# Marks of the alignment path: two accumulated TensorE products and a ScalarE copy in place of a VectorE difference and shuffle

## What is computed

```python
# 1  attention with squared scores, 16 heads of 16
A = tril((q * 0.25) @ k.T) ** 2 ;  o = (A @ v) / (A.sum(-1) + 1e-5) ;  x += o @ Wo
# 2  alignment of the context (77 rows) to the normalized x (1024 rows)
D = pairwise_euclidean(ctx, norm(x))
R[i, j] = D[i, j] + min(R[i-1, j], R[i, j-1], R[i-1, j-1])
path = backtrack(R)                 # from (76, 1023) to (0, 0): diagonal, up or left
x[j] += sum of ctx[i] over the cells (i, j) of the path
# 3  feed-forward: 256 -> 1024, two ten-stage butterflies, gelu, 1024 -> 256
x += ffn(norm(x))
```

## Time and profile before

| | us |
|---|---|
| median of three runs | 914.62 |
| the profiled execution | 919.23 |
| its span, first to last instruction | 917.5 |
| TensorE busy | 782.3 |
| VectorE busy | 489.3 |
| ScalarE busy | 446.9 |

### The profile page before, as it was taken

One profiled execution on the slowest core, in us unless ns is written; L12 is line 12 of the kernel. 1 busy time (PEld: TensorE's weight loads), 2 busy tenths in 40 slices (PEclk: granted clock), 3 DMA queues, 4 the chain that ended last, 5 costly groups with the idle time before them and its releaser, 6 DMA issues.

```text
span 917.5 us, 12051 instructions
## 1 busy us (share of the span) xinstructions
PE 782.3 (85%) x3927; PEld 384.2 (42%) x3927; DVE 489.3 (53%) x1921; ACT 446.9 (49%) x672; POOL 147.5 (16%) x332
## 2 busy tenths in 40 slices
PE   4887988799899978899988978867899972699998
PEld 3352323234333324333233322334476561457657
DVE  5637553531546122569997884239759886431000
ACT  1245776766667754778865757523412300241220
POOL 2121222221221111212222202101001000100100
PEclk9899997889999989979999989977999986799999
DMA  4481532210323220314422211101010012000001
GB/s 145 146 251 65 184 108 77 69 48 23 116 70 149 71 59 20 89 34 137 132 90 84 61 39 34 25 9 28 15 38 31 15 45 64 10 0 24 24 0 46
DMA packets 52761, 61.25 MB, mean 67 GB/s; under 512 B 21007, under 2 KB 31939, under 8 KB 52699
## 3 DMA queue, kind: packets, MB, share of 16 engines
q1 hardware_dynamic: 51611, 56.28, 20.4%
q0 software_dynamic: 1088, 4.19, 1.4%
HBM read 37.16 MB, written 23.30 MB: 66 GB/s over the span
## 4 chain that ended last, share of the span: by engine, by line
PE 57%; DVE 29%; ACT 6%; issue 5%; DMA 2%; SPq 1%; DVEq 0%; ACTq 0%
PE psO L1205 11%; PE psS L1188 10%; PE psS L1352 8%; PE psW L1362 7%; PE psW L1257 5%; DVE FOLD L917 3%; DVE STATS L1032 3%; PE psW L1248 3%; PE psW L1280 3%; ACT ARENA L778 3%; DVE FOLD L977 3%; PE psW L1264 2%; PE psW L1289 2%; DVE XX L1053 2%; PE psW L1292 2%
## 5 line engine op out<-in xcount | busy, mean ns | idle before, releaser
L778 ACT ACTIVATE ARENA<-psS 128x1024 f32<-128x1024 f32 (+3 forms) x384 | 301.0, 811 | 110.5 <-PE psS L1188 107.7
L1188 PE MATMUL psS<-ARENA 96*128 96x512 bf16 (+3 forms) x768 | 196.2, 347 | 30.5 <-ACT ARENA L778 29.5
L702 POOL TENSOR_SCALAR_AFFINE_SELECT ARENA<-ARENA 128x256 f32<-128x256 f32 x256 | 110.4, 435 | 410.3 <-ACT ARENA L778 408.6
L1205 PE MATMUL psO<-ARENA 128*32 128x512 f32 (+3 forms) x1536 | 173.2, 525 | 3.4 <-ACT ARENA L783 2.5
L1188 PEld LDWEIGHTS psS<-ARENA 96*128 96x128 bf16 x768 | 57.1, 100 | 219.3 <-ACT ARENA L778 125.7
L1362 PE MATMUL psW<-W2E,ARENA 128*128 128x256 f32 x512 | 114.6, 385 | 6.8 <-DVE ARENA L1168 6.2
L1362 PEld LDWEIGHTS psW<-W2E,ARENA 128*128 128x128 f32 x512 | 98.7, 193 | 23.0 <-DVE ARENA L1168 6.6
L845 ACT ACTIVATE ARENA<-psS,BEFF 128x512 f32<-128x512 f32 x64 | 43.5, 687 | 122.7 <-PE psS L1352 122.7
L1248 PE MATMUL psW<-IDENT,XX 128*128 128x128 f32 x192 | 36.9, 348 | 46.8 <-DVE XX L1053 46.8
L1080 DVE TENSOR_TENSOR X<-X,psW 128x512 f32<-128x512 f32 x32 | 21.7, 684 | 100.6 <-PE psW L1280 50.6
L1257 PE MATMUL psW<-XX,ARENA 128*128 128x512 f32 x128 | 68.0, 638 | 5.1 <-DVE ARENA L1068 3.1
(11 more groups left out here) (143 smaller groups left out, 817.9 us busy)
## 6 DMA issues: line engine op xcount, KB each, us to landing
ARENA<-qk_parts SPq DMA_DIRECT2D x192, 128.0 KB, 2.7
qk_parts<-ARENA SPq DMA_DIRECT2D x16, 768.0 KB, 3.7
out<-ARENA SPq DMA_DIRECT2D x16, 256.0 KB, 2.1
X<-in_x POOLq DMA_DIRECT2D x3, 1024.0 KB, 7.2
dist<-ARENA SPq DMA_DIRECT2D x1, 2560.0 KB, 8.1
MORE<-dist SPq DMA_DIRECT2D x16, 160.0 KB, 2.3
path<-MORE SPq DMA_DIRECT2D x16, 80.0 KB, 2.0
path<-FOLD SPq DMA_DIRECT2D x16, 80.0 KB, 2.2
```

Of the source, the lines that this page charges most:

```text
L702: pool.affine_select(out=blk, in_=blk, compare_op=ALU.is_ge, fill=0.0, base=0, pattern=[[0, 2], [1, P]], channel_multiplier=-1).then_inc(s ...
L778: nc.scalar.activation(A[:, (2 * G + a) % A_PAIRS, :, 0:N], psS[:, a, :, 0:N], ACT.Square).then_inc(s_sq, 1)
L1188: ins = nc.tensor.matmul(psS[:, a, j, 0:N], KST[0:STACK, g % 2, 2 * a + j, kt * P:(kt + 1) * P], QST[0:STACK, g % 2, 2 * a + j, q0:q0 + N] ...
L1205: ins = nc.tensor.matmul(psO[32 * j:32 * j + 32, o % 2, q0 - qc * HALF:q0 - qc * HALF + N], V1[:, kt, GH * g + j], A[:, (2 * G + j // 2) % ...
```

## The change

`mark` on VectorE keeps only the first of its three operations. UPTO is doubled, so that two groups alternate. A new unit `("mark", w, g)` joins the plan and `ITEM_KINDS`. TensorE multiplies UPTO with MIRRORED[:, 0] and REACH with MIRRORED[:, 1] into one psW bank, accumulating: MIRRORED is the identity for lanes 0 to 63 and reverses the blocks in each set of 32 of the other lanes, with +1 for the first and -1 for the second matrix. ScalarE copies lanes 0 to 63 as they are and lanes 64 to 127 with reversed columns into MARK, and SP sends all lanes with one DMA. TURNED goes. A `mark` unit stands four backward steps after the step that completes its group, the last one directly after it, and the late half of the path (`path(w, 1)`) is loaded after backward step 4 instead of 8. GpSimd makes MIRRORED at the start, by seven instructions.

```diff
@@ make_plan
-                      + [("backward", w, t) for t in reversed(range(early, T))] + path(w, 1)
-                      + [("backward", w, t) for t in reversed(range(early))] + path(w, 0))
+                      + flat([("backward", w, t)] + ([("mark", w, t // GRP + 1)] if t % GRP == GRP - 4 and t + GRP < T else [])
+                             + (path(w, 1) if t == GRP - 4 else []) for t in reversed(range(T))) + [("mark", w, 0)] + path(w, 0))
-ON_SCALAR = ("turn_x", "qk", "value", "turn_s", "turn_f", "dist")
+ON_SCALAR = ("mark", "turn_x", "qk", "value", "turn_s", "turn_f", "dist")
+ITEM_KINDS = (..., "out", "mark")
@@ SyncE, path_out
-                sp.wait_ge(s_path, w * T // GRP + n + 1)
-                for lanes, marks in ((slice(0, 64), MARK), (slice(64, 128), TURNED)):
-                    sp.dma_start(by_lane(path_dram, w)[lanes, g * GRP:(g + 1) * GRP], marks[lanes, n % 2]).then_inc(s_path_out[w][n % 2], 16)
+                sp.wait_ge(s_free[bank("mark", w, g)], made("mark", w, g))
+                sp.dma_start(by_lane(path_dram, w)[:, g * GRP:(g + 1) * GRP], MARK[:, n % 2]).then_inc(s_path_out[w][n % 2], 16)
@@ GpSimd, lane_tables
+                step(pool.memset(MIRRORED[:], 0.0))
+                for x in range(2):
+                    step(pool.affine_select(out=MIRRORED[0:64, x, 0:64], ..., fill=1.0 - 2.0 * x, ...))
+                    for q in range(PAIR, 2 * PAIR):
+                        step(pool.affine_select(out=MIRRORED[lanes, x, lanes], ..., fill=1.0 - 2.0 * x, base=1 - W_BLK, ...))
@@ ScalarE
+                elif kind == "mark":
+                    ...
+                    act.wait_ge(s_ready, ready(*u))
+                    marks = psW[:, bank(*u), 0:GRP * CB].rearrange("p (t c) -> p t c", t=GRP)
+                    nc.scalar.activation(MARK[0:64, n % 2], marks[0:64], ACT.Copy)
+                    nc.scalar.activation(MARK[64:128, n % 2][:, :, ::-1], marks[64:128], ACT.Copy).then_inc(s_free[bank(*u)], 1)
@@ VectorE, backward
+                if n % GRP == 0 and n >= RING:
+                    dve.wait_ge(s_ready, ready("mark", w, t // GRP + 2))
@@ VectorE, mark
-                nc.vector.scalar_tensor_tensor(out=UPTO, in0=KIND[:, rows], scalar=1.0, in1=TWO[:, r:r + GRP],
+                nc.vector.scalar_tensor_tensor(out=UPTO[:, done % 2], in0=KIND[:, rows], scalar=1.0, in1=TWO[:, r:r + GRP],
                                                op0=ALU.min, op1=ALU.is_lt).then_inc(s_upto, 1)
-                if n >= 2:
-                    dve.wait_ge(s_path_out[w][n % 2], 16 * WAYS * (n // 2))
-                dve.wait_ge(s_upto, done + 1)
-                nc.vector.tensor_tensor(out=MARK[:, n % 2], in0=UPTO, in1=REACH[:, r:r + GRP, 1:CB + 1], op=ALU.subtract).then_inc(s_mark, 1)
-                dve.wait_ge(s_mark, done + 1)
-                nc.vector.stream_shuffle(TURNED[64:128, n % 2], MARK[64:128, n % 2][:, :, ::-1], MIRROR).then_inc(s_path, 1)
@@ TensorE
+                elif kind == "mark":
+                    _, w, g = u
+                    pe.wait_ge(s_upto, w * T // GRP + T // GRP - g)
+                    r = g * GRP % RING
+                    marks = W[:, 0:GRP * CB].rearrange("p (t c) -> p t c", t=GRP)
+                    nc.tensor.matmul(marks, MIRRORED[:, 0], UPTO[:, (T // GRP - 1 - g) % 2], start=True, stop=False)
+                    ins = nc.tensor.matmul(marks, MIRRORED[:, 1], REACH[:, r:r + GRP, 1:CB + 1], start=False, stop=True)
```

More of the change, by code:

```diff
@@ L214, in make_plan @@
     return plan
-ON_SCALAR = ("turn_x", "qk", "value", "turn_s", "turn_f", "dist")
-ITEM_KINDS = ("context", "order", "w_exp", "turn_x", "qk", "value", "wo", "turn_s", "dist", "coef", "chain", "up", "w1", "down", "along", "turn_f", "out")
+ON_SCALAR = ("mark", "turn_x", "qk", "value", "turn_s", "turn_f", "dist")
+ITEM_KINDS = ("context", "order", "w_exp", "turn_x", "qk", "value", "wo", "turn_s", "dist", "coef", "chain", "up", "w1", "down", "along", "turn_f", "out", "mark")
 def layer(nc, x, ctx_in, Wq, Wk, Wv, Wo, W_exp, b_exp, up_w, up_b, down_w, W_con, b_con, down_b, out):
@@ L312, in layer @@
         PLACE = sb("PLACE", [LANES, CB + 1])
+        MIRRORED = sb("MIRRORED", [LANES, 2, LANES], BF16)
         FIRST = sb("FIRST", [LANES, CB + 1], BF16)
@@ L340, in layer @@
         TWO = view(RING * CB // 2, BF16, FOLD)[0:LANES].rearrange("p (t c) -> p t c", t=RING)
-        UPTO = view(GRP * CB // 2, BF16, FOLD)[0:LANES].rearrange("p (t c) -> p t c", t=GRP)
-        TURNED = view(2 * GRP * CB, of=FOLD)[0:LANES].rearrange("p (u t c) -> p u t c", u=2, t=GRP)
+        UPTO = view(GRP * CB, BF16, FOLD)[0:LANES].rearrange("p (u t c) -> p u t c", u=2, t=GRP)
         at[0] = 0
@@ L440, in layer @@
         s_upto = sem("s_upto")
-        s_mark = sem("s_mark")
-        s_path = sem("s_path")
         s_dsk_in = [sem("s_dsk_even"), sem("s_dsk_odd")]
@@ L567, in path_in @@
                 for i in range(2):
-                    sp.wait_ge(s_path_out[b // PAIR][i], 16 * WAYS * ((groups + 1 - i) // 2))
+                    sp.wait_ge(s_path_out[b // PAIR][i], 16 * ((groups + 1 - i) // 2))
                 for way, marks in enumerate((by_row(path_dram, b, 0), by_row_mirrored(path_dram, b))):
@@ L581, in distances @@
                         for j in range(2):
-                            sp.wait_ge(s_path_out[0][j], 16 * WAYS * ((T // GRP + 1 - j) // 2))
+                            sp.wait_ge(s_path_out[0][j], 16 * ((T // GRP + 1 - j) // 2))
                 else:
@@ L613, in _ @@
                     distances(u[1], u[2] // CH + 1)
-                elif kind == "backward" and u[2] % GRP == 0:
-                    path_out(u[1], u[2] // GRP)
+                elif kind == "mark":
+                    path_out(*u[1:])
                 elif kind == "path":
@@ L665, in lane_tables @@
                 step(pool.memset(KEEP[:], 1.0))
+                step(pool.memset(MIRRORED[:], 0.0))
+                for x in range(2):
+                    step(pool.affine_select(out=MIRRORED[0:64, x, 0:64], in_=MIRRORED[0:64, x, 0:64], compare_op=ALU.not_equal,
+                                            fill=1.0 - 2.0 * x, base=0, pattern=[[-1, 64]], channel_multiplier=1))
+                    for q in range(PAIR, 2 * PAIR):
+                        lanes = slice(32 * q, 32 * q + 32)
+                        step(pool.affine_select(out=MIRRORED[lanes, x, lanes], in_=MIRRORED[lanes, x, lanes], compare_op=ALU.not_equal,
+                                                fill=1.0 - 2.0 * x, base=1 - W_BLK, pattern=[[1, 32]], channel_multiplier=1))
                 for q in range(PAIR * WAYS):
@@ L754, in _ @@
                     nc.scalar.activation(SD[:, t0:t1], VE[:, t0:t1], ACT.Sqrt).then_inc(s_sd, 1)
+                elif kind == "mark":
+                    _, w, g = u
+                    n = T // GRP - 1 - g
+                    if n >= 2:
+                        act.wait_ge(s_path_out[w][n % 2], 16 * (n // 2))
+                    elif n == 0 and w:
+                        act.wait_ge(s_row, 2 * (T + 1))
+                    act.wait_ge(s_ready, ready(*u))
+                    marks = psW[:, bank(*u), 0:GRP * CB].rearrange("p (t c) -> p t c", t=GRP)
+                    nc.scalar.activation(MARK[0:64, n % 2], marks[0:64], ACT.Copy)
+                    nc.scalar.activation(MARK[64:128, n % 2][:, :, ::-1], marks[64:128], ACT.Copy).then_inc(s_free[bank(*u)], 1)
                 elif kind == "turn_x":
@@ L885, in warp_start @@
                 if w == 0:
-                    dve.wait_ge(s_lanes, 2 + 4 * PAIR * WAYS)
+                    dve.wait_ge(s_lanes, 9 + 4 * PAIR * WAYS)
+                if w:
+                    dve.wait_ge(s_ready, ready("mark", w - 1, 0))
                 vec(nc.vector.memset(ROWS[:, 0], BIG))
@@ L985, in mark @@
                 rows, r = slice(g * GRP, (g + 1) * GRP), g * GRP % RING
[L986 to L989, removed]
-                nc.vector.scalar_tensor_tensor(out=UPTO, in0=KIND[:, rows], scalar=1.0, in1=TWO[:, r:r + GRP],
-                                               op0=ALU.min, op1=ALU.is_lt).then_inc(s_upto, 1)
-                if n >= 2:
-                    dve.wait_ge(s_path_out[w][n % 2], 16 * WAYS * (n // 2))
-                dve.wait_ge(s_upto, done + 1)
-                nc.vector.tensor_tensor(out=MARK[:, n % 2], in0=UPTO, in1=REACH[:, r:r + GRP, 1:CB + 1], op=ALU.subtract).then_inc(s_mark, 1)
-                dve.wait_ge(s_mark, done + 1)
-                nc.vector.stream_shuffle(TURNED[64:128, n % 2], MARK[64:128, n % 2][:, :, ::-1], MIRROR).then_inc(s_path, 1)
+                done = w * T // GRP + T // GRP - 1 - g
+                nc.vector.scalar_tensor_tensor(out=UPTO[:, done % 2], in0=KIND[:, rows], scalar=1.0, in1=TWO[:, r:r + GRP],
+                                               op0=ALU.min, op1=ALU.is_lt).then_inc(s_upto, 1)
             for u in plan:
```

## The result

The changed kernel takes 954.7 us (median of 4 executions, 946.27 to 955.25) against 914.5 for the kernel before: the ratio is 1.040, 95% interval 1.035 to 1.045, which on 914.6 us is 36.6 us. The profiled execution took 954.35 us with a span of 952.6, so 35.1 us more than the profiled one of before, at a mean granted clock of 0.91. The forecast was 947 with a range of 932 to 957: the sign and the mechanism hold, the size is 8 us short.

A forecast was written before the change was run, and what follows sets the result against it. VectorE was taken to bound the second warp, while TensorE and VectorE held each other in the first. Second warp +23.8 and first warp +9.2 gave 33 us on the median 914.6: 947 us, range 932 to 957.

The forecast's parts named there:

- The lead at mark 7: TensorE reaches mark 7 before UPTO is ready and stands still 17 us in the second warp, 9 in the first.
- VectorE's saving: VectorE loses 1.11 us in each group, 8 times in a warp: 9 us.
- Rival (a): VectorE stays the bound and gets faster, as TensorE comes to each mark after UPTO: 906 us; chance 5%.
- The mark's own price: Each mark: two products on TensorE, some 0.45 us, and two copies on ScalarE, some 0.9 us.
- First warp: +9.2 us, between +4 and +12: mark 7 +7, marks 6 to 4 +2, VectorE -1.8, marks 2 to 0 +2.
- Rival (b): The first warp absorbs its wait in later idle times, leaving +2: 940 us; chance 15%.
- Second warp: Wait at mark 7, rounds of `out` and marks, then the end: `along` +23.8 us later, between +18 and +28.
- the price of the clock in the ring: Second warp: idle time in each round may lower TensorE's clock, 0 to 2.9 us; 1.4 taken each, 4.3 in all.
- the ring: Second warp: each `out` waits for addition, four steps, UPTO and mark: 11.3 us a round, three times, 33.9 us.
- the tail: Second warp's end: addition 0.8, steps 2.5, UPTO 0.5, mark 0.5, ScalarE 1.0, then 7.7 us to `along`.
- rival (d): Every restart is cold and first-warp marks cost their ScalarE time in full: 956 us; chance 15%.
- Rival (c): Second warp: TensorE could start out 1 before mark 3 is filled, about +10; with first warp +9, 934 us; chance 10%.

The follow-up runs named there:

- e1: Changed kernel with all added work in place, but mark products read a constant table, so TensorE does not wait for VectorE there: 921.62 us, ratio 1.0068.
- e3: Changed kernel with each mark eight backward steps behind its group instead of four, in both warps: 926.93 us, ratio 1.0134.
- e4: Changed kernel with REACH holding all 64 rows, UPTO written over KIND and marks placed later in both warps: 916.44 us, ratio 1.0015.
- e5: Kernel before, with the mark's difference and shuffle left out and nothing in their place: 906.53 us, ratio 0.9886.
- e7: e4 with the second warp's outs and marks spread over the backward steps: 914.16 us, ratio 0.9949.
- the corners: Changed kernel with TensorE's mark waits removed in both warps, first only, second only, or neither: ratios 1.0068, 1.0322, 1.0133, 1.0400 to the kernel before.
- e9: e7 with the first warp's marks and path_in back at the changed kernel's places, four steps behind: 916.49 us, ratio 0.9975.
- e6: Changed kernel with unread filler products on TensorE ahead of second-warp marks 7, 3, 2, 1 and 0: 946.97 us, ratio 1.0334.

## Why the prediction was right, and where it was short

**The lead at mark 7: right.** Forecast waits of 17 and 9 us; 16.05 and 8.76 measured, each ended by VectorE's L1007. e1, e3 and e4 show by three different edits that the position is what costs.

**VectorE's saving: right in size, wrong in what it would be worth.** e5 has `along` 11.8 us earlier, 3.1 of them already at the start of `hidden` (694.92), so 8.7 in the second warp against the 9 of the forecast. Rival (a) had this mechanism and took its gain to reach `along`; e4 shows that without waits at marks most of it is still lost on SyncE's queue, and e7 gets back about half a per cent.

**The mark's own price: right.** 0.45 us on TensorE forecast; at the full clock the two products of 0.30 start 0.13 to 0.14 apart, so 0.43 to 0.44 from start to end. Two copies: 0.9 forecast from the rows, 0.86 measured. The 1.13 us by the Trainium skill's "ScalarE: Activation LUTs", "Rules for kernel authors", was not borne out; that row is for an activation whose bias is a pointer operand, and these copies name no bias.

**First warp: +9.2 forecast, +8.3 in the trace,** 6 to 7 by the corners. The sum is nearer than its terms. `value` 2 begins at 495.60, 5.4 us late where 7 were taken; the transposes that began at 534.29 before begin at 538.97, 4.7 late where 7.2 were forecast (7, +2, -1.8); from there on 3.6 are added where 2 were forecast. Too much and too little partly cancel, which is luck. The last part isn't a wait for VectorE: from these transposes to `hidden` it is 163.7 us before and 162.5 in e5, and 167.2 to 171.8 in all eleven traces with marks on TensorE, e1 (167.7) among them. Two of TensorE's waits for ScalarE there grew from 1.19 and 1.80 us before to 2.17 and 2.38 in e1; where the rest arises is not shown. Rival (b), absorbed to 2 us, fails in every trace that keeps these marks four steps behind; only the median of e9 comes near it, and why is open.

**Second warp: +23.8 forecast, +26.0 in the trace,** 23 to 24 by the corners. By steps, the first 8.3 us of shift taken off: `out` 0 ends at 752.8 (forecast 754.4), 1.6 less; from its addition at 761.16 to the last at 801.50 are 40.3 us (38.2), 2.1 more; from there to `along` 14.5 (13.0), 1.5 more. **The step that was too small is the price of the clock in the ring**: 1.4 us a round was taken as half of the range from 0 to 2.9; the rows give 1.7, 2.4 and 2.4 (`out` at 8.77, 9.51 and 9.45 against 7.09), and e6 takes it away. After 3.79 us of idle time the clock did fall, where the earlier trace rows had shown it stay after 2.84. The Trainium skill, "TensorE: Matmul & The Clock Gate", "HAM oscillation", had it on this side: waits between bursts let the clock fall and the next burst starts cold. The trace agrees in the direction: granted clocks of 0.81, 0.74 and 0.75 in the three `out`s behind a wait, though each cost less than the 2.9 us that the two `out`s of the earlier trace rows had lost. In the tail, from ScalarE's second copy to `along` it is 9.1 us where 7.7 were forecast: the last `path_out` was held 2.26 us behind four `path_in`, where 1.7 or nothing had been averaged:

```profile
802.71 3.89 SPq L568 DMA_DIRECT2D ARENA<-path  x4
806.93 2.26 SPq L554 DMA_DIRECT2D path<-MORE  x1
```

**The sum.** 33 was forecast for the trace and 34.3 is found at `along`; no step of the two traces shows the rest, up to the 36.6 of the ratio and the 40 of the medians; the spread between executions (946.27 to 955.25) is as large. The time ended near rival (d), 956. Its first half, that every restart is cold, is what happened, at 1.7 to 2.4 us in the ring instead of 2.9; its second, marks of the first warp at their full ScalarE time, is not what the corners show: e1, which keeps all the copies, has its `hidden` at 701.56, only 3.5 us late. Rival (c), no ring, is e3 made true: 926.9, 7 us better than its 934, as e3's first warp lost 2.0 us and not 9.

**What e1 keeps.** From `hidden` to `along` its second warp takes 81.7 us, 2.0 less than before (83.8), where e5, with VectorE's saving alone, takes 75.1. By the trace the 6.7 us between them are the turn of the banks, the rival named in its expectation: `out` 1 waits 6.36 us for the addition of `out` 0, and the next ones begin 9.9 and 8.0 us apart, each behind an addition, so that the last addition ends at 769.6 and not at 760.7 as before. With the first warp's 3.5 this is why e1 isn't faster than the kernel before.

**Where an even first warp would lead** was not forecast: in e7 TensorE reaches the transposes of the last norms at 525.78 and before at 534.29, yet `hidden` begins at 697.55 and 698.03. Between 564 and 600 the granted clock was 0.81 in e7 and 0.95 before (the second line), which may account for a part of it; in e1 it was 0.95 too, and the stretch was still 4 us longer than before. No run here tells whether the clock is cause or company.

```profile
564.00:600.00 36.00, 28.08 (x140) 12.14 (x140) 9.36 (x26) 17.89 (x27) 3.27 (x8) 0.81 0.18 35
564.00:600.00 36.00, 28.64 (x168) 11.72 (x167) 10.77 (x30) 20.42 (x29) 4.06 (x10) 0.95 0.13 23
```

## What to carry to other kernels

Before a small operation moves from a lagging engine into the queue of one that runs ahead, compare when each engine reaches that place in the plan: the lead, not the duration, is the price, and everything queued behind pays it. If the receiving engine also feeds the sender (here `out` to the addition), put more sender steps between the value and its reader than one exchange takes; here four steps made a ring, eight opened it and were worth 24 us over both warps. Look at the shared banks too: one unit put between two others can move them onto the same bank, which here made a ring of 7.97 us a round by itself. When the bottleneck then gets faster, follow its last result through the DMA queue to the first reader before counting the gain.

## What the runs showed of the hardware beyond the forecast

- After each idle time of 3.79 us TensorE began 32 products at 1.2 GHz for a part of them: 8.77, 9.51 and 9.45 us against 7.09, at granted clocks of 0.81, 0.74 and 0.75; of the second and third the first 2.8 and 3.0 us stand at 0.50. With the gap filled by products that nobody reads, 7.09 each time, at 1.00.
- On SyncE, one issue directly behind four `path_in` was held 2.25 to 2.56 us in e4, e7 and the kernel after (in the kernel before the one of L621, 2.55), where an issue alone takes 0.3 to 0.5; eight in a row took 9.80 us, against 3.56 for four.
- The same kernel differs by 13 us between executions (e7: 904.23 to 917.25 for ten of twelve), with a mean granted clock of 0.941 in the fastest and 0.925 in the slowest, so that half a per cent can't be told from a few executions.
